# Splitting the weight builds between VectorE and ScalarE with GpSimd, and issuing all second-layer builds in one run

## What is computed

```python
def _L0_ffn_ref(x, gate_w1, gate_b1, gate_w2, gate_b2, W1, b1, W2, b2, TW1, Tb1, TW2, Tb2):
    h = relu(x @ gate_w1.T + gate_b1)
    g = (h @ gate_w2.T + gate_b2).mean(axis=1)          # 8 numbers per sequence
    mW1 = W1 + einsum('be,efh->bfh', g, TW1)            # TW1: 8 x 4096 x 1024
    mW2 = W2 + einsum('be,ehf->bhf', g, TW2)            # TW2: 8 x 1024 x 4096
    u = gelu(einsum('bsh,bfh->bsf', x, mW1) + mb1)
    return einsum('bsf,bhf->bsh', u, mW2) + mb2

xn = layernorm(x)                                       # x: 4 x 4096 x 1024
out = x + attention(xn) + _L0_ffn_ref(xn, ...)          # 8 heads, window of 16
```

## Time and profile before

| | us |
|---|---|
| median of 2 runs | 3455.77 (3454.81 to 3456.72) |
| the profiled execution | 3467.81 |
| its slowest core (5): first to last instruction | 3466.0 |
| fastest core (0) | 3389.7 |
| busy: PE / DVE / ACT / POOL | 1224.9 / 972.7 / 365.9 / 5.5 |
| DMA read and written | 475.33 MB, mean 137 GB/s |

### The profile page before, as it was taken

How to read it: one execution, slowest core, us unless ns; L and a number is a source line. 1 busy time by engine, 2 the same in 40 slices (tenths; PEclk the granted TensorE clock), 3 DMA queues, 4 the chain that set the end, 5 groups by cost and what they waited for, 6 DMA issues and landing times.

```text
span 3466.0 us, 17506 instructions; the slowest of 8 cores (3389.7 to 3466.0 us)
## 1 busy us (share of the span) xinstructions
PE 1224.9 (35%) x5044; PEld 494.3 (14%) x5044; DVE 972.7 (28%) x943; ACT 365.9 (11%) x755; POOL 5.5 (0%) x11
## 2 busy tenths in 40 slices
PE   0332422652362335325431430210102037657474
PEld 0111111221121112101210110000000012222131
DVE  1111120135225523551454125344443410000000
ACT  1121110310120022002110110000000002010010
POOL 0000000000000000000000000000000000000000
PEclk9776766875685577558665665555555568989798
DMA  9223123016506532561356557878879764464544
GB/s 194 67 58 90 50 66 52 0 50 217 140 8 213 190 111 72 189 209 53 127 200 206 136 163 247 206 225 200 222 221 206 210 157 90 91 134 88 125 92 109
DMA packets 466034, 475.33 MB, mean 137 GB/s; under 512 B 362579, under 2 KB 362963, under 8 KB 465812
## 3 DMA queue, kind: packets, MB, share of 16 engines
q1 hardware_dynamic: 345060, 248.90, 27.2%
q10 hardware_dynamic: 116400, 214.81, 21.6%
q0 software_dynamic: 4480, 10.50, 1.9%
HBM read 357.91 MB, written 42.01 MB: 115 GB/s over the span
## 4 chain that ended last, share of the span: by engine, by line
DMA 34%; PE 25%; DVE 18%; SPq 6%; ACT 6%; issue 6%; ACTq 4%; DVEq 1%
DMA O_s<-TW 23%; DVE accv_s L90 9%; SPq L95 6%; PE pA L74 6%; DMA O_s<-m2d 5%; PE pC L74 5%; PE pB L74 5%; PE pU L74 4%; ACTq L95 4%; PE pD L74 3%; DVE rz_s L90 3%; PE pE L74 2%; DMA O_s<-xad 2%; DVE mwov_s L90 2%; DMA xnd<-xnb_s 2%
## 5 line engine op out<-in xcount | busy, mean ns | idle before, releaser
L90 DVE SCALAR_TENSOR_TENSOR accv_s<-O_s,gbc_s,accv_s 128x1024 f32<-128x1024 f32 x448 | 575.3, 1284 | 715.5 <-DMA O_s<-TW 689.4
L74 PE MATMUL pA<-O_s 128*128 128x512 bf16 x640 | 205.0, 443 | 850.3 <-DMA O_s<-m2d 599.9
L74 PEld LDWEIGHTS pA<-O_s 128*128 128x128 bf16 x640 | 66.8, 108 | 988.3 <-issue 945.8
L74 PE MATMUL pU<-rz_s,e0f_s 128*128 128x512 f32 x64 | 59.0, 1077 | 377.5 <-DVE rz_s L90 377.5
L74 PE MATMUL pB<-O_s 128*128 128x512 bf16 x640 | 187.7, 410 | 0.0
L85 ACT ACTIVATE O_s<-pA,mb_s 128x512 bf16<-128x512 f32 x64 | 44.0, 687 | 1254.8 <-PE pA L74 1254.7
L90 DVE TENSOR_TENSOR O_s<-pA,O_s 128x512 f32<-128x512 f32 x4 | 2.8, 692 | 574.8 <-PE pU L74 574.8
L74 PE MATMUL pC<-gb1r_s,e0bf_s 128*128 128x512 bf16 x32 | 13.9, 435 | 341.6 <-DMA xt_s<-xnd 334.8
L90 DVE TENSOR_SCALAR_CACHE_REDUCE junk_s<-O_s 128x1024 f32<-128x1024 f32 x32 | 38.8, 1214 | 321.4 <-ACT hrelu_s L85 320.7
L90 DVE RECIPROCAL rz_s<-pE 1x512 f32<-1x512 f32 x32 | 104.8, 3311 | 72.6 <-PE pE L74 72.6
L74 PE MATMUL pE<-O_s 128*128 128x512 bf16 (+1 forms) x384 | 116.7, 361 | 0.0
(11 more groups left out here) (135 smaller groups left out, 1337.7 us busy)
## 6 DMA issues: line engine op xcount, KB each, us to landing
O_s<-TW SPq DMA_DIRECT2D x256, 512.0 KB, 5.6
O_s<-TW ACTq DMA_DIRECT2D x256, 512.0 KB, 7.5
O_s<-x SPq DMA_DIRECT2D x16, 1024.0 KB, 5.6
accv_s<-W SPq DMA_DIRECT2D x32, 512.0 KB, 4.0
accv_s<-W ACTq DMA_DIRECT2D x32, 512.0 KB, 5.5
xnd<-xnb_s ACTq DMA_DIRECT2D x32, 256.0 KB, 2.8
O_s<-x ACTq DMA_DIRECT2D x16, 512.0 KB, 3.8
xad<-O_s ACTq DMA_DIRECT2D x16, 512.0 KB, 2.6
```

The lines of the kernel that those rows point to most:

```text
L74: i = self.eng.matmul(out, lhsT, rhs, start=start, stop=stop, skip_group_check=skip)
L90: i = getattr(self.eng, name)(*args, **kw) if self.on(who) else None
```

## The change

- Groups alternate by `par = bld_n % 2`. Even groups: loads and store issued by ScalarE, eight multiply-adds on VectorE as before. Odd groups: loads and store issued by SyncE; for each of eight terms ScalarE computes `tmp = slot * g` (`Identity` with a scale, 128x1024 float32 in, bf16 out, into `bldt0` or `bldt1` in turn) and GpSimd adds `tmp` to `acc` (`tensor_tensor`). The slot is free when ScalarE's instruction is done. ScalarE's term e waits for GpSimd's add e - 2.
- All 32 mW2 groups are emitted before the `ft` loop of sc = 0, not eight before each quarter.

```diff
-        q = "sync" if m1 else "scalar"
+        q = "scalar" if par == 0 else "sync"
+        lsem = "v" if par == 0 else "p"
-        cx.wait_at(q, "v", bk["acc_done"][par])
+        asem, acnt = bk["acc_done"][par]
+        cx.wait_at(q, asem, acnt)
         cx.dma(q, acc, wsrc, wdsem)
@@ the eight loads
             elif e < 4:
-                cx.wait_at(q, "v", bk["mac_cnt"][i - 4])
+                ms, mc = bk["mac_cnt"][i - 4]
+                cx.wait_at(q, ms, mc)
             else:
-                cx.wait_at(q, "v", v0 + (e - 4) + 1)
+                cx.wait_at(q, "v" if par == 0 else "a", base + (e - 4) + 1)
@@ the eight terms; par == 0 keeps the multiply-adds on vector
+            else:
+                tmp = s["bldt0"] if e % 2 == 0 else s["bldt1"]
+                cx.wait_at("scalar", ds, dc)
+                pw = bk["pool_e"].get(e - 2 if e >= 2 else e + 6, 0)
+                if pw:
+                    cx.wait_at("scalar", "p", pw)
+                cx.act(tmp, slots[i % 4], AF.Identity, scale=s["gbc"][:, e:e + 1])
+                bk["mac_cnt"][i] = ("a", cx.cnt["a"])
+                cx.wait_at("gpsimd", "a", cx.cnt["a"])
+                if e == 0:
+                    cx.wait_at("gpsimd", wsem, wcnt)
+                cx.wait("gpsimd", "p")
+                if e == 7 and bk["out_sem"][par] is not None:
+                    osm, ocn = bk["out_sem"][par]
+                    cx.wait_at("gpsimd", osm, ocn)
+                cx.vop("tensor_tensor", out, tmp, acc, op=ALU.add, who="gpsimd")
+                bk["pool_e"][e] = cx.cnt["p"]
-        cx.wait_at(q, "v", done)
+        cx.wait_at(q, lsem, done)
         cx.dma(q, dst, outbuf, osem)
@@ emit_ffn
+            if sc == 0:
+                emit_vector_builds(cx, 64)
             for ft in range(32):
-                if sc == 0 and ft % 8 == 0:
-                    emit_vector_builds(cx, 8)
```

More of the change, by code:

```diff
@@ L168, in build_program @@
         ("accv2", (128, D), F32), ("mwov2", (128, D), BF16),
+        ("bldt0", (128, D), BF16), ("bldt1", (128, D), BF16),
     ]:
@@ L437, in emit_build_group @@
         i0 = bk["bld_idx"]
-        v0 = cx.cnt["v"]
+        base = cx.cnt["v" if par == 0 else "a"]
         for e in range(8):
@@ L454, in emit_build_group @@
             ds, dc = bk["slot_dma"][i]
[L455 to L459, removed]
-            out = acc if e < 7 else outbuf
[L461 to L465, removed]
@@ L466, in emit_build_group @@
-            bk["mac_cnt"][i] = cx.cnt["v"]
+            out = acc if e < 7 else outbuf
+            if par == 0:
+                cx.wait_at("vector", ds, dc)
+                if e == 0:
+                    cx.wait_at("vector", wsem, wcnt)
+                    cx.wait_at("vector", "a", bk["gbc_a"])
+                cx.wait("vector", "v")
+                if e == 7 and bk["out_sem"][par] is not None:
+                    osm, ocn = bk["out_sem"][par]
+                    cx.wait_at("vector", osm, ocn)
+                cx.vop("scalar_tensor_tensor", out, slots[i % 4],
+                       s["gbc"][:, e:e + 1], acc, op0=ALU.mult, op1=ALU.add)
+                bk["mac_cnt"][i] = ("v", cx.cnt["v"])
+            else:
[7 more added lines that the diff above has]
+                cx.wait_at("gpsimd", "a", cx.cnt["a"])
+                if e == 0:
+                    cx.wait_at("gpsimd", wsem, wcnt)
+                cx.wait("gpsimd", "p")
+                if e == 7 and bk["out_sem"][par] is not None:
+                    osm, ocn = bk["out_sem"][par]
+                    cx.wait_at("gpsimd", osm, ocn)
+                cx.vop("tensor_tensor", out, tmp, acc, op=ALU.add, who="gpsimd")
+                bk["pool_e"][e] = cx.cnt["p"]
@@ L467, in emit_build_group @@
         bk["bld_idx"] = i0 + 8
-        done = cx.cnt["v"]
-        bk["acc_done"][par] = done
-        cx.wait_at(q, "v", done)
+        done = cx.cnt[lsem]
+        bk["acc_done"][par] = (lsem, done)
+        cx.wait_at(q, lsem, done)
         cx.dma(q, dst, outbuf, osem)
@@ L970, in body @@
                     "bld_n": 0, "bld_idx": 0, "slot_dma": {}, "mac_cnt": {},
-                    "acc_done": {0: 0, 1: 0}, "out_sem": {0: None, 1: None},
+                    "acc_done": {0: ("v", 0), 1: ("p", 0)},
+                    "out_sem": {0: None, 1: None}, "pool_e": {},
                     "vq": 0, "hraw_a": [], "qraw_a": [], "kstt_v": [], "ppa": [],
@@ L980, in body @@
                 full_schedule(c)
+                if os.environ.get("K_CNT"):
+                    print("LANE", name, {k: v for k, v in c.cnt.items() if v})
             return body
```

## The result

The changed kernel takes **3622.85 us** (median) against 3457.95 in the same comparison: ratio 1.0483 (95% interval 1.045 to 1.0516), 165 us slower by the medians and 167 by the ratio. (In some executions of each kernel one die runs at a lower clock and the time is longer: the medians here are of all executions, the ratios of the undisturbed ones.) The forecast was 3566, range 3461 to 3700, slower. Sign and range held; the loss is half as large again as the +110 of the sum.

A forecast was written before the change was run, and what follows sets the result against it. The prediction took the builds to run at the pace of loads, no engine full. Its terms, 147 + 29 + 5 - 144 + 73 = +110, gave 3578 us on the profiled execution, 3566 as median, range 3461 to 3700.

The forecast's parts named there:

- GpSimd's add: Odd groups: a 128x1024 add takes 2.3 us plus 0.1 between dependent adds, and sets the odd group's pace.
- 19 us for 0.1: All odd groups: each 0.1 us of a term moves 0.6 us in 31 places, 19 us in all.
- Inside a chunk: Attention, 11 tile periods: each grows from 56.4 to 69.8 us, +13.4, together +147 us.
- B's first slots ... are there: Attention tile: the odd group's first slots are loaded during the even group, so its first term starts at 19.9 us.
- Front: Attention tile: work formerly under VectorE's builds now follows the odd group's terms uncovered, 8.3 us with a hop.
- Over a turn: Between chunks, three times: the `xt` transposes stand behind ScalarE's odd-group terms, +9.7 us each, +29 in all.
- First layer: Last tile and first layer of sc = 0: 187 us from t0 to the last gelu against 181.4, +5.
- mW2 builds: The 32 mW2 groups: 16 pairs of 38.2 us make 611 against 755.6 us, interference included, -144.
- Second layer exposed: Second layer of sc = 0: all 32 steps follow the builds, 100 us against 27.2, +73.
- No quicker for two queues: Rival, builds: a pair still takes 43.2 us though loads overlap; 3646 us, chance 0.13.
- Quick and slow adds: Rivals, odd groups: adds at 1.28 + 0.1 us give 3467 us, chance 0.12; at 3.31 + 0.1, 3759 us, chance 0.12.
- The faster case: Rival, builds: quick adds and loads without a gap bring a pair to 30 us; 3372 us, chance 0.04.

The follow-up runs named there:

- the shorter adds: The changed kernel with seven of eight GpSimd adds per odd group cut to 256 of 1024 columns: 3551.9 us, ratio 1.0278 to the kernel before.
- the late stores: The kernel before, with each group's store issued behind the first four TW loads of the next group: 3380.7 us, ratio 0.9766.
- the first experiment: The changed kernel with 14 odd groups emitted inside the next tile, behind its sums and ahead of the reciprocals: 3344.7 us, ratio 0.966 to the kernel before.
- all mW1 loads on SyncE: The changed kernel with all mW1 loads and stores issued by SyncE, arithmetic still split: 3636.9 us, ratio 1.053 to the kernel before.

## Point by point: where the prediction held and where it failed

- **GpSimd's add.** Taken as 2.3 + 0.1 from the middle of wide bounds; it is 2.13 + 0.15 = 2.28. The estimate from the Trainium skill (GPSIMD Engine Reference, "Performance versus the Vector engine"), 2.25 for the add alone, was a little closer than 2.3, and the trace (2.13) agrees with it to 0.12. By my own 19 us for 0.1 this is worth -23 us; the shorter adds bear out that rate only as far as the loads allow.
- **Inside a chunk: +13.4 forecast, +16.0 measured** (mean core). This term was mis-sized, 29 us in 11 periods. The parts of the tile above against the steps: even group to 20.4 after t0 (19.3 forecast). "B's first slots ... are there" was wrong: the first was asked for at 1241.0 and read at 1247.0, so the first term starts at 22.3 and not 19.9. Terms 16.2 (16.7). Front 9.9 (8.3): I priced it from a row in which TensorE had just run the output projection, at the higher clock; see the last section. Reciprocal to t0 23.6 (24.8).
- **Over a turn: +9.7 forecast, +8.2 measured.** Held.
- **First layer: +5 forecast**, +9.1 on a mean core (203.5 to 212.6); on the slowest cores of the two profiles, last reciprocals to last gelu is 204.7 before and 216.2 after, +11.5. SyncE's eight `xnd` transposes take 18.4 us beside group 30's loads (10.1 in the earlier trace rows), which I had not counted.
- **mW2 builds: -144 forecast.** After: 621.6 on the profiled core, 611 forecast, a pair 38.8 and not 38.2. What failed is the other side of the subtraction. I took 755.6, that of the slowest core, and it had the longest builds of all eight: they range from 702 to 756, mean 726.5, while after they lie at 613 to 624. On a mean core the gain is 108. Slow builds and slow attention are on different cores before (core 3 has the longest attention, core 5 the longest builds), so shortening only the builds of core 5 does not shorten the chip's time by as much: with every core's builds at the mean, core 3 (3456.7, builds 731) would end last, at about 3452. This is the largest error, 36 us.
- **Second layer exposed: +73 forecast**; on the profiled cores 103.0 after against 27.2, +75.8; on a mean core 97.5 against 26.8, +71. Held.
- **Rivals.** "No quicker for two queues" fell: DMA share 0.83 at 255 GB/s, pair 38.8 us. The sentence of the Trainium skill (DMA: Bandwidth & Descriptors, "Issuing engines are not separate DMA queues") is not contradicted, since the late stores get 284 GB/s from one queue: what helps is that slots are asked for without a gap. Quick and slow adds fell by the row of the add. The faster case fell.

The forecast named the reason of the loss, the cover lost by the front, and the first experiment bears it out. It took the position of the odd groups as given, though, and did not see that the loss had a cheap cure: the same work emitted one step later is 7.7% faster.

By the sum, on a mean core: forecast +110; the tile +29, the turn -5, the first layer +4, the builds +36 and the second layer -2 make +172. The start (-8) and the last chunks (-4), which the forecast left at nothing, bring it to the measured +160; the median moved by 165.

## What to carry to other kernels

Work moved to an idle engine also moves into that engine's queue: list what stands behind it there (here the exponentials, the transposes, and a "wait for everything of ScalarE" on TensorE), and put it where that engine waits anyway. Before adding arithmetic engines to a loop that waits for loads, ask first whether the loads are asked for early enough. With a time that is the slowest core's, take each stage's baseline from all cores, not from the slowest one.

## What the runs showed of the hardware

A GpSimd `tensor_tensor` add of 128x1024 (bf16 and float32 in) takes 2133 ns, 128x256 takes 670: a line through the two is 1.9 ns a column and 0.2 us fixed. With adds running beside them (the odd groups inside the tile), VectorE's two reciprocals take 6.56 us, as they do alone.

512 KB loads slow the DMA transposes beside them: issuing eight transposes takes 10.1 to 10.7 us without loads beside them and 15.5 to 25.0 beside them (the late stores, all mW1 loads on SyncE).

The front's TensorE part, windows of before (first line, from the bias matmuls of the scores on) and after (second line, from the `selbf` matmuls on; third line, its first 2 us):

```profile
1094.20:1098.00 3.80, 3.70 (x20) 1.74 (x20) 3.59 (x3) 1.06 (x2) 0.00 (x0) 1.00 0.72 224
...
1263.30:1269.00 5.70, 5.57 (x22) 1.90 (x22) 0.00 (x0) 1.06 (x2) 3.08 (x2) 0.73 0.27 73
1263.30:1265.30 2.00, 1.94 (x5) 0.30 (x6) 0.00 (x0) 0.83 (x2) 1.80 (x2) 0.50 0.03 8
```

Before, this part follows directly on the output projection and runs at a granted clock of 1.00 (2.4 GHz). After, TensorE has stood idle for 40 us in front of it and starts at the lower level (0.50, 1.2 GHz; the mean of the stretch is 0.73). The 20 matmuls from the bias ones on take 4.6 us (1264.31 to 1268.94) where they took 3.7, and the two of `selbf` about 0.95 with their hop where I had priced 0.6: 1.3 of the 1.6 us that the front was mis-sized by. The work that was moved behind a wait was also moved to the lower clock.
